# Counting two units in a row on TensorE, with three pairs of PSUM banks, in a recommender kernel that pools by matmul

## What is computed

```
x = mlp(dense_x, bottom)                       # 2048 x 13 -> 512 -> 256 -> 64, relu
pooled = tables[t][indices[t]].sum(axis=1)     # 26 tables, 2048 samples, 20 rows of 64 each
Tcat = concat(x, pooled)                       # 2048 x 27 x 64
Z = einsum('bim,bjm->bij', Tcat, Tcat)         # pairwise products
y = mlp(concat(x, Z[lower triangle]), top)     # 415 -> 512 -> 256 -> 1, sigmoid at the end
```

## Time and profile before

| | |
|---|---|
| median of three runs | 3051.23 us (3049.17 to 3052.97) |
| the profiled execution | 3058.61 us, span 3056.8 us |
| mean granted TensorE clock | 0.963 of full speed |
| TensorE (matmul) busy | 2934.3 us, 96% of the span |
| ScalarE busy | 2182.6 us, 71% |
| VectorE busy | 1991.5 us, 65% |
| GpSimd busy | 1759.3 us, 58% |
| chain that ended last | PE 85%, ACT 7%, issue 5% |

### The profile page before, as it was taken

The page is one execution under the profiler, slowest core; times in us unless marked ns, Lnnn a source line. Parts: engine busy times, 40 slices in busy tenths (PEclk is TensorE's granted clock), DMA queues, the critical chain, the costliest instruction groups (busy, mean ns, idle before and its releaser), DMA issues.

```text
span 3056.8 us, 65500 instructions
## 1 busy us (share of the span) xinstructions
PE 2934.3 (96%) x24204; PEld 1249.3 (41%) x24204; DVE 1991.5 (65%) x3358; ACT 2182.6 (71%) x2496; POOL 1759.3 (58%) x1640
## 2 busy tenths in 40 slices
PE   6999999999999999999999999999999999999798
PEld 2333343333433333333333333333333333337574
DVE  4477676776767767677676776767767677643221
ACT  3678778777777777877778778777777877872232
POOL 3266676666766667676676666766667676300000
PEclk8899999999999999999999999999999999997668
DMA  2112122121221212212122121221212212007711
GB/s 66 59 29 72 28 72 70 29 72 27 73 69 29 71 28 73 69 30 71 28 73 69 30 71 27 73 69 29 71 28 73 69 30 69 17 25 119 129 35 29
DMA packets 173103, 167.99 MB, mean 55 GB/s; under 512 B 116105, under 2 KB 134329, under 8 KB 167477
## 3 DMA queue, kind: packets, MB, share of 16 engines
q1 hardware_dynamic: 121380, 110.94, 13.2%
q0 software_dynamic: 51200, 52.53, 8.7%
q10 hardware_dynamic: 272, 0.52, 0.1%
HBM read 143.83 MB, written 20.05 MB: 54 GB/s over the span
## 4 chain that ended last, share of the span: by engine, by line
PE 85%; ACT 7%; issue 5%; SPq 1%; DMA 1%; DVE 0%; ACTq 0%; POOL 0%; DVEq 0%; POOLq 0%
PE ps L678 59%; PE ps L659 16%; PE ps L624 5%; PE ps L745 4%; ACT counts L820 4%; ACT parts L782 2%; ACT parts L789 1%; SPq L496 0%; ACT h_bot L833 0%; ACT pooled_sb L811 0%; SPq L519 0%; DMA look_in<-in_r_indices 0%; DMA pooled<-pooled_sb 0%; DMA products<-zt 0%; SPq L503 0%
## 5 line engine op out<-in xcount | busy, mean ns | idle before, releaser
L598 POOL DMA_INDIRECT rows<-in_L_rec_tables,look x1600 | 1745.2, 1091 | 834.3 <-issue 474.2
L820 ACT CAST counts<-ps 128x792 int32<-128x792 f32 (+1 forms) x1848 | 1773.0, 979 | 583.3 <-PE ps L659 571.1
L678 PE MATMUL ps<-counts,parts 128*128 128x512 fp8e3 x8232 | 2178.4, 390 | 0.0
L1037 DVE TENSOR_TENSOR onehot_p<-iota_by_unit,place 128x1024 bf16<-128x1024 bf16 x924 | 636.6, 689 | 639.1 <-PE ps L659 613.4
L678 PEld LDWEIGHTS ps<-counts,parts 128*128 128x128 f16 x8232 | 646.8, 96 | 755.6 <-issue 6.2
L659 PEld LDWEIGHTS ps<-onehot_c,onehot_p 60*128 60x128 bf16 x14448 | 382.4, 95 | 876.1 <-issue 758.2
L659 PE MATMUL ps<-onehot_c,onehot_p 60*128 60x99 bf16 x14448 | 666.5, 209 | 55.0 <-ACT counts L820 35.2
L1042 DVE TENSOR_TENSOR onehot_c<-column_c,weighted_s 128x792 bf16<-128x792 bf16 x924 | 521.7, 565 | 0.0
L1071 DVE TENSOR_REDUCE rows<-rows 128x64 f32<-128x384 f32 (+1 forms) x240 | 188.1, 784 | 9.0 <-DVE pooled_sb L1048 9.0
L998 DVE SCALAR_TENSOR_TENSOR raw<-raw,coef_next,parts 128x896 f32<-128x896 f32 x147 | 168.4, 1146 | 18.1 <-ACT parts L782 18.1
L381 DVE COPY zt<-ps 32x208 f32<-32x208 f32 x128 | 64.8, 507 | 152.4 <-PE ps L745 150.5
(11 more groups left out here) (82 smaller groups left out, 525.4 us busy)
## 6 DMA issues: line engine op xcount, KB each, us to landing
raw<-in_L_rec_tables SPq DMA_DIRECT2D x21, 1792.0 KB, 8.3
raw<-in_L_rec_tables SPq DMA_DIRECT2D x21, 1344.0 KB, 11.8
rows<-in_L_rec_tables,look POOLq DMA_INDIRECT x1600, 2.5
pooled<-pooled_sb SPq DMA_DIRECT2D x84, 128.0 KB, 2.3
slots<-pooled SPq DMA_DIRECT2D x30, 352.0 KB, 7.9
products<-zt SPq DMA_DIRECT2D x16, 351.0 KB
idx_raw<-in_r_indices SPq DMA_DIRECT2D x42, 79.7 KB
gathered<-bags_t SPq DMA_DIRECT2D x42, 64.0 KB
```

What stands on the lines that cost most here:

```text
L598: nc.gpsimd.indirect_dma_start(rows[:, s, l, :], None, rows_flat, bass.IndirectOffsetOnAxis(ap=look[:, c, s * PL + l:s * PL + l + 1].bitca ...
L678: mm = nc.tensor.matmul(acc[k % 2][:, 0:NB], parts[:, j, :], count_bytes[k % 2][:, j % COLS, 0:NB, j // COLS], start=(j == 0), stop=(j == ...
L820: nc.scalar.copy(counts[k % 2][:, :, u * UG * GS:(u * UG + g) * GS].rearrange("p c (g h s) -> p h g c s", h=HALVES, s=HS), unit_ps[u % 2][ ...
L1037: tt(onehot_p[:, r, :, :, :], iota, at, ALU.is_equal)
```

## The change

Four things change together.

1. `phase` runs over pairs: units u and u+1 are counted one behind the other, and eight sums follow. After the last pair 18 sums are left (8 and 10), before it was 14.
2. There are three pairs of PSUM banks for counts, banks 0 to 5. A unit now waits until the unit three before it is unpacked. As 88 units do not divide by three, the last unit of a table takes buffer 1, and the wait counts from a table of buffers.
3. The sums move to banks 6 and 7. Indices and bags no longer have banks of their own: indices go to bank 6 in phase 1 (before unit 10), while that phase sums in bank 7, and bags to bank 7 in phase 0 (before unit 10), while that phase sums in bank 6. TensorE has new waits: on `acc_free` before each of the two, on `bags_copied` before phase 1 and on `idx_copied` before phase 2. The first table's indices use bank 4. The bottom perceptron has two banks.
4. On ScalarE `convert_indices` and `copy_bags` change places and come after units 10 and 12. On VectorE `copy_indices` moves from pair 2 to pair 6 of block 2, `find_partition` and `find_field` from pairs 3 and 5 of block 2 to pairs 1 and 5 of block 3, and the chunks of the maximum are spaced a little differently.

```diff
-        unit_ps = [ps[:, 2 * i:2 * i + 2, 0:UG * HC] for i in range(2)]
-        acc = banks[4:6]
-        idx_ps, bags_ps = banks[6], banks[7]
-        bot_banks = [banks[4], banks[5], banks[7]]
+        unit_ps = [ps[:, 2 * i:2 * i + 2, 0:UG * HC] for i in range(3)]
+        acc = banks[6:8]
+        idx_ps, first_idx_ps, bags_ps = acc[0], banks[4], acc[1]
+        bot_banks = banks[6:8]
...
+        ROUND_UNITS = BLOCKS * UNITS
+        buffer_of = [i % 3 for i in range(ROUND_UNITS - 1)] + [1]
...
             def turn_indices(t, first=False):
                 pe.wait_ge(idx_converted, 3 * t + 3)
                 if not first:
-                    pe.wait_ge(idx_copied, t)
+                    pe.wait_ge(acc_free, BLOCKS * (t - 1) + 3)
...
             def turn_bags(n, done):
                 pe.wait_ge(piece_free, PIECES + PIECES * done)
+                pe.wait_ge(acc_free, BLOCKS * n + 2)
...
-                if not (first and u < 2):
-                    pe.wait_ge(counts_ready, n - 1)
+                if not (first and u < 3):
+                    pe.wait_ge(counts_ready, n - units_since(k, u) + 1)
...
-                for u in range(UNITS):
-                    if bags and u == 6:
+                for u in range(0, UNITS, 2):
+                    if bags and u == 10:
                         turn_bags(t, GB * t)
-                    j1 = SPAN if u == UNITS - 1 else PER_UNIT * (u + 1)
+                    if indices and u == 10:
+                        turn_indices(t + 1)
+                    j1 = SPAN if u == UNITS - 2 else PER_UNIT * (u + 2)
                     await_rows(t, k, PER_UNIT * u, j1)
                     count_unit(tn, kn, u)
-                    for j in range(PER_UNIT * u, PER_UNIT * (u + 1)):
+                    count_unit(tn, kn, u + 1)
+                    for j in range(PER_UNIT * u, PER_UNIT * (u + 2)):
                         sum_rows(t, k, j)
...
                 phase(t, 0, t, 1, bags=True)
-                turn_indices(t + 1)
-                phase(t, 1, t, 2)
+                pe.wait_ge(bags_copied, t + 1)
+                phase(t, 1, t, 2, indices=True)
+                pe.wait_ge(idx_copied, t + 2)
                 phase(t, 2, t, 3)
```

More of the change, by code:

```diff
@@ L372, in build, with unit_buffer, units_since @@
         PER_UNIT = 4
+        ROUND_UNITS = BLOCKS * UNITS
+        assert ROUND_UNITS % 3 == 1
+        buffer_of = [i % 3 for i in range(ROUND_UNITS - 1)] + [1]
+        def unit_buffer(k, u):
+            return buffer_of[(k * UNITS + u) % ROUND_UNITS]
+        def units_since(k, u):
+            i = k * UNITS + u
+            return next(d for d in range(1, ROUND_UNITS) if buffer_of[(i - d) % ROUND_UNITS] == buffer_of[i])
         def take_diagonals(eng, copy, b, quarters, done):
@@ L630, in turn_indices @@
                 if not first:
-                    pe.wait_ge(idx_copied, t)
+                    pe.wait_ge(acc_free, BLOCKS * (t - 1) + 3)
+                into = first_idx_ps if first else idx_ps
                 for k in range(BLOCKS):
-                    last = nc.tensor.transpose(idx_ps[:, k * GROUPS:(k + 1) * GROUPS], idx_f[:, k, :],
+                    last = nc.tensor.transpose(into[:, k * GROUPS:(k + 1) * GROUPS], idx_f[:, k, :],
                                                ident[0:GROUPS, 0:GROUPS])
@@ L658, in count_unit @@
                         rows_h = slice(h * HP, h * HP + HK)
-                        last = nc.tensor.matmul(unit_ps[u % 2][:, h, x * HC:(x + 1) * HC],
+                        last = nc.tensor.matmul(unit_ps[unit_buffer(k, u)][:, h, x * HC:(x + 1) * HC],
                                                 onehot_p[rows_h, r, sub, :, lane],
@@ L684, in sum_rows, with phase @@
                     mm.then_inc(chunk_used, 1)
[L686 to L689 removed]
+            def phase(t, k, tn, kn, bags=False, indices=False):
+                for u in range(0, UNITS, 2):
+                    if bags and u == 10:
                         turn_bags(t, GB * t)
[L691 removed]
+                    if indices and u == 10:
+                        turn_indices(t + 1)
+                    j1 = SPAN if u == UNITS - 2 else PER_UNIT * (u + 2)
                     await_rows(t, k, PER_UNIT * u, j1)
                     count_unit(tn, kn, u)
[L694 removed]
+                    count_unit(tn, kn, u + 1)
+                    for j in range(PER_UNIT * u, PER_UNIT * (u + 2)):
                         sum_rows(t, k, j)
@@ L716, in _ @@
             for k in range(BLOCKS - 1):
+                if k == 1:
+                    pe.wait_ge(bags_copied, TP)
                 phase(TP - 1, k, TP - 1, k + 1, bags=k == 0)
@@ L859, in unpack_block1 @@
                         make_lo(t, CHUNKS - 3 + (u - 4) // 2)
-                    elif u == 10:
+                    elif u == 10 and t is not TP - 1:
+                        convert_indices(t + 1)
+                    elif u == 12:
                         copy_bags(t)
-                    elif u == 12 and t is not TP - 1:
-                        convert_indices(t + 1)
             with act.Fori(0, TP - 1) as t:
@@ L922, in copy_indices @@
                     dve.wait_ge(idx_ready, t)
-                nc.vector.tensor_copy(idx_t[:, :], idx_ps[:, 0:NI]).then_inc(idx_copied, 1)
+                nc.vector.tensor_copy(idx_t[:, :], (first_idx_ps if first else idx_ps)[:, 0:NI]).then_inc(idx_copied, 1)
             ts = nc.vector.tensor_scalar
@@ L1128, in _ @@
                     if d == 2:
-                        copy_indices(t + 1)
                         max_chunk(t + 1, 0)
-                    elif d == 3:
-                        find_partition(t + 1)
                     elif d == 4:
                         max_chunk(t + 1, 1)
[L1135 to L1138, removed]
+                    elif d == 6:
+                        copy_indices(t + 1)
+                        max_chunk(t + 1, 2)
+                    elif d == 7:
+                        max_chunk(t + 1, 3)
                     elif d == 8:
@@ L1148, in _ @@
                     onehot_pair(t, 3, d)
-                    if d == 3:
+                    if d == 1:
+                        find_partition(t + 1)
+                    elif d == 3:
                         pool_bags(t, 1)
+                    elif d == 5:
+                        find_field(t + 1)
                     elif d == 7:
```

4 lines of the change are left out of this document (2 added, 2 removed).

## The result

The changed kernel takes 2881.19 us in the median (2880.54 to 2882.4), beside 3051.02 before: a ratio of 0.9444 with a 95% interval of 0.9427 to 0.946. The forecast was 2887.

What follows compares the result with a forecast made beforehand. TensorE, busy 96% of the span, was taken as the bound. Twenty tables at -8.2 us (-164), the last -6.3 and clock +6 gave -164 together: median 2887 us, range 2862 to 2940, faster 0.95.

Steps and rivals of the forecast that it cites:

- The bursts: TensorE, each pair: grouped bursts and sums save 0.205 us, 2.25 a phase; full phases go from 30.84 to 28.6.
- the two equal gaps: TensorE: gaps into and out of the sums are equally long, only one has a wait; second burst 0.20 us, not 0.30.
- half the switch: Rival: the second unit's wait costs a new start, 0.10 us a pair; 2974 us, chance 0.07.
- the sequencer is caught out: Rival: TensorE's sequencer can't run ahead past the register instruction between bursts; slower, 3090 us, chance 0.03.
- Phase 0: Start of phase 0: unchanged VectorE chain through `take_lo` holds unit 4 until 6.95 us, stall +0.41 a table.
- Phase 3: Waits for ScalarE in pairs 8, 9 and 10: 0.86 us of stalls instead of 0.28, +0.58 a table.
- The follower's case: Rival: ScalarE in phase 3 and VectorE in phase 1 can't go faster; 82 us lost, 2969 us, chance 0.08.
- The loop's end: TensorE's 1.00 us gap at the loop's end: -0.3 us a table taken, bounds 0 and -1.0.
- The total: Sum of terms -164 us: profiled execution from 3058.6 to 2894.6, median 2887 us, 5.4% less.
- Phase 1: VectorE behind the moved `copy_indices`: +0.1 us a table; pair 9 tightest, one-hots ready at 21.7, wanted at 22.0.
- The clock: Granted clock drops after phase 0's longer stall: 10 of 20 phases instead of 6, +6 us in all.
- Start and end: Bottom perceptron at the start with two banks, not three: 0 taken, bounds a gain of 5 us and 19 us.

Runs made afterwards that it cites:

- e1: Changed kernel with one count burst and four sums again, the other parts of the change kept: 3045.96 us, ratio 0.9968.
- e2: Kernel before with only the pairs of bursts and eight sums, two pairs of PSUM banks and old places kept: 2937.74 us, ratio 0.9617.
- e4: Changed kernel with VectorE writing three pairs of one-hots ahead, not two (`AHEAD = 3`): 2847.83 us, ratio 0.9324.
- e6: Kernel before with VectorE writing three pairs of one-hots ahead, not two: 3024.47 us, ratio 0.9909.
- e8: Changed kernel with ScalarE's hi and lo steps of phase 3 later and further apart: 2862.43 us, ratio 0.9368.
- e5: Changed kernel with the last two units, 20 and 21, counted apart, so 14 sums stand behind the last count: 2896.03 us, ratio 0.949.
- e3: Changed kernel with `find_partition` and `find_field` on VectorE back in block 2, behind pairs 7 and 8: 2927.83 us, ratio 0.9579.
- e10: Changed kernel with three pairs of one-hots ahead, later phase 3 hi and lo steps, and three-unit bursts in phases 1 and 2: 2891.11 us, ratio 0.9475.

## Why the prediction was right

**The bursts.** The second burst was to cost 0.20 us, at worst 0.30. It costs 0.20, and a full phase is 28.54, where 28.6 was said. The argument from the two equal gaps held, so *half the switch* is out, and so is *the sequencer is caught out*. The register instruction between the bursts costs nothing that a row shows. e1 and e2 show that this is the source of the gain: without the bursts 0.3%, with them alone 3.8%. What TensorE does in the 0.10 us on the way in and the 0.11 on the way out, no run shows; only that they are paid per change. The Trainium skill (TensorE: Matmul & The Clock Gate, "Wait — 56ns, not 53.3ns?") gives 62 ns a matmul with hardware decode off, by which the second eight would have needed an estimated 0.50 us. They took 0.20, so this price does not hold for this program; how its matmuls are decoded, no run shows.

**Phase 0.** The chain was to hold unit 4 until 6.95 us; it does until 6.98, and e4 and e6 show that it is this chain. Phase 0 fell by 2.00 us in the median, 2.14 being its share of the sum (2.25 less 0.41, and the indices' 0.3 gone to phase 1). The added 0.41 does not all stand ahead of unit 4, as I had said: in the mean of 20 tables unit 2 starts 0.37 late, where it was 0.14 (in the timeline 0.32, for nothing that the trace shows), and the idle time ahead of unit 4 went from 1.51 to 1.71.

**Phase 3.** The waits were placed on pairs 8, 9 and 10 and sized 0.43, 0.26 and 0.17; they are there, at 0.48, 0.31 and 0.19. e8 shows their cause. The follower's case did not come about.

**The loop's end** was the term that was mis-sized most: the step "I take -0.3, nearer to no change because a full queue holds it back alike". The gap fell from 0.82 in the median to 0.10, so by 0.7, nearer to the bound of one us than to my 0.3; e5 shows that the sums behind the last count do it. That fits a sequencer that reaches the branch earlier by most of the 0.9 us that four sums last; no trace here shows when it reached it.

**The total.** The forecast lacked 6 us in the median, but 14 for the traced execution (2894.6 against 2880.54). By the traces, the gap gave 8 us more than the sum had, full phases 4 (2.30 each, not 2.25), two clock drops fewer 4, VectorE in phase 1 and the start and end 2 each; phase 3's waits took 2 of it back and phase 0 took 3. That only 6 show in the median is luck: I took 7.4 us off because the traced execution of the kernel before lay that far above its median, while the changed kernel's lies at its own (2880.54 beside 2881.19).

**Phase 1.** +0.1 a table was allowed for VectorE; it cost nothing. Its one-hots of pair 9 are ready at 1236.61 in the timeline and counted at 1236.88, with no wait: 0.27, where 0.3 was worked out. Of that, 0.14 is what a count takes from ready one-hots in the earlier trace rows, so the true room is about 0.13.

```profile
1236.05 0.56 DVE L1063 TENSOR_TENSOR onehot_c<-column_c,weighted_s 128x792 bf16<-128x792 bf16 x1
```
```profile
1236.88 0.56 PE L674 MATMUL ps<-onehot_c,onehot_p 60*128 60x99 bf16 x16
```

e3 shows that without the move this would be a wait of 1.94.

**The clock.** Ten drops were assumed and eight came. I had argued that a longer stall meets the drop more often. Within the change's trace the idle times of TensorE ahead of unit 4 agree; between kernels they do so only in part. Here is one with a drop behind it in the change, and one of e5 without:

```profile
951.35 0.57 PE L674 MATMUL ps<-onehot_c,onehot_p 60*128 60x99 bf16 x16 [1.86 <-ACT counts L841]
```
```profile
1077.51 0.56 PE L674 MATMUL ps<-onehot_c,onehot_p 60*128 60x99 bf16 x16 [1.64 <-DVE onehot_c L1064]
```

In the change, the eight drops follow idle times of 1.75 to 1.92 us; three phases with 1.83 have no drop, and none of the ten with less than 1.75 has one. In e5 unit 4 comes as late after the first count, but more of the wait stands ahead of unit 2 (unit 2 at 2.97 us in the mean, in the change at 2.77). So the idle time ahead of unit 4 is 1.50 in the mean, not 1.71, and over 1.70 in two phases alone; e5 has no drop. Length alone does not decide, though: the kernel before has 1.51, the same as e5, and six drops, e3's 1.93 in phase 1 was followed by a drop in 8 of 20 tables, e10's 1.74 to 1.77 in 19. What else does, the runs don't say. The number of drops also differs between executions of one kernel: the traced execution before, with six, had a mean granted clock of 0.963 and took 3058.61 us; others at 0.968 took 3050 to 3055. So six is probably high for the kernel before, and the change probably loses more to the clock than the 2 us between the two traces.

**Start and end** fell by 2 us together (115.98 to 115.46 us ahead of the first sum, 281.0 to 279.4 from the last sum on), so two banks for the bottom perceptron cost nothing that shows; other runs with the same two banks start 115.4 to 118.6 us in, so 3 us could hide there.

## What to carry to other kernels

Where two kinds of matmul with different row extents alternate, read the cost of the change from a short burst and a long one (four counts against eight, four sums against fourteen); it hides in busy time, and grouping pays it half as often. Before grouping, lay the queues of the engines that fill and drain the bursts side by side: a second pair of buffers carried the gain where they had no other work, and the third, with the moves that made room for it, was worth 53 us with the grouping and 10 without. Then look at the stalls that the grouping leaves as they are; here one constant on VectorE and two lists on ScalarE gave another 51 us.

## What the runs showed of the hardware

- A change of TensorE between counts of 60 rows and full sums costs 0.10 us on the way in and 0.11 on the way out, inside its busy time: half as many changes took a full phase from 30.84 to 28.54 us, and for the same matmuls 178 us of busy time went.
- The gap of TensorE at the turn of the loop depends on how many sums stand behind the last count: with 14 it is 0.82 us in the median (before), 0.96 (e1) and 0.73 (e5), with 18 it is 0.10 (the change) and 0.20 (e2).
- An idle time of TensorE of 1.65 to 2.2 us at the upper clock of 2.4 GHz was followed in some tables by some 3 us at the lower one of 1.2: in 6 of 20 tables (before), 8 (the change), 5 (e8), 8 (e3, phase 1), 19 (e10) and none (e5). In none of the traces did a drop in the loop follow a shorter idle time; what else decides is open. A drop costs 1.4 to 1.6 us, nearly as much again as the stall itself.
- GpSimd's 1600 gathers took 1118 ns in the mean, 1091 before, by a trace that is rough on GpSimd. No run separates why. Their waits for VectorE, 359.4 us in the earlier trace rows, fell to 161 us in the same stretch of the loop, and no wait of TensorE is put down to GpSimd.
